# A graph network's own products moved into the aggregation, with input tiles and one-hots rearranged

## The reference

```python
x = ln(x + gcn_block(x))                 # W, degree norm, batch norm over nodes, gelu, + x
x = ln(x + sage(sage(x)))                # relu(h @ Ws + mean_of_neighbours(h) @ Wn + b), twice
x = ln(x + rgcn(relu(rgcn(x))))          # agg over edges of sigmoid(x_j @ gate_r) * x_j @ w_r, + x @ root + bias
x = ln(x + (relu((x + agg(x)) @ W1 + b1) @ W2 + b2))
# rgcn weights: w = einsum('rb,bio->rio', att, basis), 2 relations, 30 bases of 512 x 512
```

## Time and profile before

| | before |
|---|---|
| median of 3 runs, us | 933.22 (931.15 to 935.43) |
| the profiled execution, us | 935.52 |
| its span in the profile, us | 933.7 |
| TensorE matmul busy | 888.9 (95%) |
| VectorE busy | 668.8 (72%) |
| ScalarE busy | 280.8 (30%) |
| GpSimd busy | 85.5 (9%) |
| HBM read, written, MB | 97.80, 12.52 |

### The profile page before, as it was taken

How to read it: one execution, slowest core, us unless ns; L and a number is a source line. 1 busy time by engine, 2 the same in 40 slices (tenths; PEclk the granted TensorE clock), 3 DMA queues, 4 the chain that set the end, 5 groups by cost and what they waited for, 6 DMA issues and landing times.

```text
span 933.7 us, 12912 instructions
## 1 busy us (share of the span) xinstructions
PE 888.9 (95%) x4258; PEld 428.9 (46%) x4258; DVE 668.8 (72%) x1405; ACT 280.8 (30%) x431; POOL 85.5 (9%) x66
## 2 busy tenths in 40 slices
PE   7989999979987999989999899999999999999997
PEld 3544555535545544434444344444444444444443
DVE  6868888847996789798999988995324245552347
ACT  0323444633953213424132211113411131032321
...
GB/s 264 311 171 141 176 171 194 179 128 211 194 111 139 152 228 161 197 247 173 183 116 104 167 153 166 129 120 12 26 79 32 1 57 115 89 66 47 36 66 234
DMA packets 134889, 129.50 MB, mean 139 GB/s; under 512 B 80687, under 2 KB 81156, under 8 KB 134826
## 3 DMA queue, kind: packets, MB, share of 16 engines
...
...
HBM read 97.80 MB, written 12.52 MB: 118 GB/s over the span
## 4 chain that ended last, share of the span: by engine, by line
PE 61%; DVE 18%; DMA 7%; issue 5%; ACT 4%; DVEq 3%; POOL 1%; ACTq 0%; SPq 0%
PE Dp L667 25%; PE Dp L697 24%; PE T L621 6%; DVE acc L1252 4%; DMA stage<-in_basis 3%; PE Dp L573 3%; DVE Zraw L1141 2%; DMA wst<-mixd 2%; DVE Zraw L1140 1%; DVE Zraw L1363 1%; ACT W L1011 1%; PE T L667 1%; DVEq L1140 1%; ACT wst L864 1%; DVE w L1381 1%
## 5 line engine op out<-in xcount | busy, mean ns | idle before, releaser
L667 PE MATMUL Dp<-W,hT 128*128 128x512 f16 x792 | 176.2, 381 | 3.8 <-DMA hT<-S 3.8
L697 PE MATMUL Dp<-Zraw,A 128*128 128x512 f16 x800 | 173.0, 379 | 0.0
L1252 DVE SCALAR_TENSOR_TENSOR acc<-stage,att,acc 128x512 f32<-128x512 f32 x232 | 163.6, 769 | 6.2 <-DMA stage<-in_basis 6.2
L697 PE MATMUL Dp<-Zraw,AT 128*128 128x512 f16 x600 | 130.3, 379 | 0.3 <-DVE Zraw L1321 0.2
L667 PEld LDWEIGHTS Dp<-W,hT 128*128 128x128 f16 x792 | 77.7, 98 | 97.5 <-DMA hT<-S 4.6
L697 PEld LDWEIGHTS Dp<-Zraw,A 128*128 128x128 f16 x800 | 78.3, 98 | 94.4
L1141 DVE TENSOR_SCALAR Zraw<-hT,w 128x640 f16<-128x640 f16 (+1 forms) x209 | 96.4, 461 | 0.8 <-issue 0.7
L697 PEld LDWEIGHTS Dp<-Zraw,AT 128*128 128x128 f16 x600 | 58.6, 98 | 71.6 <-DVE Zraw L1321 0.7
L573 PE MATMUL Dp<-Zraw 128*128 128x320 f16 (+1 forms) x418 | 67.1, 307 | 9.2 <-DVE Zraw L1141 9.1
L1140 DVE TENSOR_SCALAR Zraw<-hT,w 128x128 f16<-128x128 f16 (+1 forms) x209 | 59.3, 284 | 22.1 <-issue 15.7
L1381 DVE SCALAR_TENSOR_TENSOR w<-Dp,aggc,S 128x512 f32<-128x512 f32 x40 | 29.9, 747 | 59.6 <-PE Dp L697 53.6
...
## 6 DMA issues: line engine op xcount, KB each, us to landing
...
```

The costliest lines, as they stand in the source:

```text
L667: last = nc.tensor.matmul(dense_bank(u, t, m), turned[:, hp, k * P:(k + 1) * P], weights_of(u, m)[:, wp, k, :], start=(n == 0), stop=(n == ...
L697: last = nc.tensor.matmul(sum_bank(t), a[:, k, ds(t * P, P)], Z[:, r, h, k, :], start=(n == 0), stop=(n == count - 1))
L1252: last = v.scalar_tensor_tensor(part, stage[:, q, :], a, part, ALU.mult, ALU.add)
```

## The change

1. Units 2 and 3 get `own_late`. Their own product leaves the dense part and is done tile by tile at the head of each tile's aggregation (`own_sum`, 12 matmuls into one of two banks of `T`). For it each tile is transposed a second time, into two slots (`fara`, `farb` in unit 2; `xra`, `xrb`, the residual's buffers, in unit 3), issued by ScalarE in `ln_step` or `relu_step`. VectorE adds the bias in `own_term`, in `after_agg`.
2. The basis quarters are dealt out anew: dense 2 from 18 to 8, agg 2 from 0 to 10, dense 3 from 35 to 24, agg 3 from 18 to 29.
3. In agg of unit 3 the maxima and scales of unit 4 are one tile later, as are the three `high` steps, so that the last one stands behind tile 9. The loads of biases 4 and 5 come one part later.
4. The input tiles are loaded one behind every two mixes instead of every three.
5. The low one-hots of a window's four fixed chunks are one instruction (`lows_of`), from an f16 copy of the low indices.
6. Transposed tiles 2 and 3 of unit 0 go to `xra` and `xrb` and no longer wait for the last mix; ScalarE issues them at the last window. One VectorE instruction (`eye`) waits on another semaphore.

The diff, cut to the changed lines and, in most places, the line ahead of them:

```diff
@@ -38,8 +38,8 @@
     dict(mats=["Wn1", "Ws1"], nz=1, own=1, zexp=18, bias="b1", ln=False),
-    dict(mats=["Wn2", "Ws2"], nz=1, own=1, zexp=24, bias="b2", ln=True),
-    dict(mats=["mix0", "mix1", "root1"], nz=2, own=2, zexp=18, bias="rb1", ln=False),
+    dict(mats=["Wn2", "Ws2"], nz=1, own=1, zexp=24, bias="b2", ln=True, own_late=True),
+    dict(mats=["mix0", "mix1", "root1"], nz=2, own=2, zexp=18, bias="rb1", ln=False, own_late=True),
@@ -157,8 +157,9 @@
         w_c = [zview(4 * NWIN).bitcast(f32) for _ in range(2)]
-        zview(2 * (2 * NT * D) - (2 * (KEYS + P) * (2 * OH + MORE) + 5 * 4 * NWIN))
+        lo_h = zview(2 * CHUNKS)
+        zview(2 * (2 * NT * D) - (2 * (KEYS + P) * (2 * OH + MORE) + 5 * 4 * NWIN + 2 * CHUNKS))
@@ -240,13 +241,14 @@
         s_wlo = sem("s_wlo")
-        s_hT = {n: sem(f"s_hT_{n}") for n in ("a", "b", "w1a", "w1b", "mida", "midb", "fara", "farb", "wsta", "wstb", "stga", "stgb")}
+        s_hT = {n: sem(f"s_hT_{n}") for n in ("a", "b", "w1a", "w1b", "xra", "xrb", "fara", "farb", "wsta", "wstb", "stga", "stgb")}
         s_own = {u: sem(f"s_own{u}") for u in (1, 2, 3, 4)}
+        s_od = sem("s_od")
@@ -330,14 +332,13 @@
             ("dense", 2, 8): [("load", 3, 2)],
-            ("agg", 2, 0): [("bias", 4)],
             ("agg", 2, 1): [("high", 3, 2)],
-            ("dense", 3, 1): [("gates", 2)],
+            ("dense", 3, 1): [("bias", 4), ("gates", 2)],
             ("dense", 3, 8): [("load", 4, 2)],
-            ("agg", 3, 1): [("bias", 5)],
-            ("agg", 3, 6): [("high", 4, 0)],
-            ("agg", 3, 7): [("high", 4, 1)],
-            ("agg", 3, 8): [("high", 4, 2)],
+            ("agg", 3, 7): [("high", 4, 0)],
+            ("agg", 3, 8): [("high", 4, 1)],
+            ("agg", 3, 9): [("high", 4, 2)],
+            ("dense", 4, 1): [("bias", 5)],
@@ -358,8 +359,8 @@
             ("agg", 3, 0): [("most", 4, 2)],
-            ("agg", 3, 5): [("most", 4, 0), ("most", 4, 1), ("max", 4)],
-            ("agg", 3, 6): [("scales", 4)],
+            ("agg", 3, 6): [("most", 4, 0), ("most", 4, 1), ("max", 4)],
+            ("agg", 3, 7): [("scales", 4)],
@@ -378,9 +379,10 @@
             ("agg", 1): [2, 2, 1, 1, 1, 2, 1, 2, 1, 1],
-            ("dense", 2): [1, 1, 2, 2, 2, 2, 2, 2, 2, 2],
-            ("dense", 3): [3, 4, 3, 4, 3, 4, 3, 4, 3, 4],
-            ("agg", 3): [4, 4, 4, 4, 2, 0, 0, 0, 0, 0],
+            ("dense", 2): [0, 1, 1, 1, 1, 1, 1, 1, 1, 0],
+            ("agg", 2): [1] * NT,
+            ("dense", 3): [2, 3, 2, 2, 3, 2, 2, 3, 2, 3],
+            ("agg", 3): [5, 4, 4, 4, 4, 4, 4, 0, 0, 0],
@@ -403,15 +405,16 @@
         far = Zraw[:, 4 * NT * D - 4 * D:]
-        mid = Zraw[:, 3 * NT * D:3 * NT * D + 4 * D]
-        HT_SLOT = {"mida": halves_view(mid[:, 0:2 * D]), "midb": halves_view(mid[:, 2 * D:]), "a": hT[:, 0], "b": hT[:, 1], "fara": halves_view(far[:, 0:2 * D]), "farb": halves_view(far[:, 2 * D:])}
-        for n, buffer in (("w1", w1), ("wst", wst), ("stg", stage)):
+        HT_SLOT = {"a": hT[:, 0], "b": hT[:, 1], "fara": halves_view(far[:, 0:2 * D]), "farb": halves_view(far[:, 2 * D:])}
+        for n, buffer in (("w1", w1), ("xr", xr), ("wst", wst), ("stg", stage)):
                 HT_SLOT[n + side] = halves_view(buffer[:, i, :].bitcast(f16))
-        HT_RING = {0: ["w1a", "w1b", "mida", "midb", "a", "b"], 2: ["a", "b", "fara", "farb"], 3: ["a", "b", "wsta", "wstb"],
+        HT_RING = {0: ["w1a", "w1b", "xra", "xrb", "a", "b"], 2: ["a", "b", "fara", "farb"], 3: ["a", "b", "wsta", "wstb"],
                     for u in range(NU) for t in range(NT)}
+        OWN_LATE = [u for u in range(NU) if UNITS[u].get("own_late")]
+        HT_NAMES.update({(u, NT + t): {2: "far", 3: "xr"}[u] + "ab"[t % 2] for u in OWN_LATE for t in range(NT)})
@@ -451,17 +454,17 @@
                 sp.dma_start(attp[b2 * 64:(b2 + 1) * 64, :], att1[b2:b2 + 1, :].broadcast_to([64, BASES])).then_inc(e_att, 16)
-            def load_mix(g, first=0, end=PAIRS):
-                for b in range(first, end):
-                    n = g * PAIRS + b
+            def load_mix(first, end):
+                for n in range(first, end):
+                    g, b = divmod(n, PAIRS)
-            load_mix(0, 0, MIX_FIRST)
+            load_mix(0, MIX_FIRST)
             sp.dma_start(src_i, src_t).then_inc(e_edge, 16)
-            load_mix(0, MIX_FIRST)
+            load_mix(MIX_FIRST, PAIRS)
@@ -470,12 +473,11 @@
             for t in range(NT):
-                load_mix(1 + t // 5, 3 * (t % 5), 3 * (t % 5) + 3)
+                load_mix(PAIRS + 2 * t, PAIRS + 2 * t + 2)
                 sp.dma_start(tile[:, :], vec).then_inc(s_bn, 16)
-            for mix_group in range(3, GROUPS):
-                load_mix(mix_group)
+            load_mix(PAIRS + 2 * NT, PAIRS * GROUPS)
@@ -640,7 +642,8 @@
             for u, unit in enumerate(UNITS):
-                nm, nz = len(unit["mats"]), unit["nz"]
+                own_late = unit.get("own_late", False)
+                nm, nz = len(unit["mats"]) - own_late, unit["nz"]
@@ -654,7 +657,7 @@
                         wait(pe, s_v, NT * LN.index(u) + t - 1)
-                    elif unit["own"] is not None:
+                    elif unit["own"] is not None and not own_late:
@@ -685,7 +688,9 @@
                     wait(pe, s_pre[u], bank_before(t))
-                    if unit["own"] is not None and t < 6:
+                    if own_late:
+                        own_sum(t)
+                    elif unit["own"] is not None and t < 6:
@@ -698,6 +703,21 @@
                     last.then_inc(s_agg[u], 1)
+                def own_sum(t):
+                    name = HT_NAMES[u, NT + t]
+                    pe.wait_ge(s_hT[name], 16 * (len(hT_before(u, NT + t)) + 1))
+                    wait(pe, s_own[u], t - 1)
+                    if t == 0:
+                        pe.wait_ge(s_wlo, halves_split(u))
+                    n, m = 0, unit["own"]
+                    for hp, wp in ((0, 0), (1, 0), (0, 1)):
+                        for k in range(KT):
+                            last = nc.tensor.matmul(T[:, t % 2, :], HT_SLOT[name][:, hp, k * P:(k + 1) * P],
+                                                    weights_of(u, m)[:, wp, k, :], start=(n == 0), stop=(n == 3 * KT - 1))
+                            n += 1
+                    last.then_inc(s_od, 1)
@@ -790,6 +810,8 @@
                             turned_out(t - 1, g, count_bank(t - 1, g))
+                    if w == NWIN - 1:
+                        turn_to(4, 0)
@@ -811,15 +833,19 @@
-                for t in range(turned[u], min(end, NT)):
+                count = 2 * NT if u in OWN_LATE else NT
+                for t in range(turned[u], min(end, count)):
                     slot = HT_NAMES[u, t]
-                    act.wait_ge(s_ready, NT * u + t + 1)
+                    act.wait_ge(s_ready, NT * u + min(t + 1, NT))
                     for before, tile in hT_before(u, t)[-1:]:
-                        act.wait_ge(s_d, NT * before + tile + 1)
-                    if slot[:2] == "w1" and t < 2:
+                        if tile < NT:
+                            act.wait_ge(s_d, NT * before + tile + 1)
+                        else:
+                            act.wait_ge(s_od, NT * OWN_LATE.index(before) + tile - NT + 1)
+                    if u == 3 and t in (NT, NT + 1):
+                        act.wait_ge(s_v, NT * (LN.index(2) + 1))
+                    if slot[:2] in ("w1", "xr") and t < 4:
                         act.wait_ge(s_ready, NT)
-                    elif slot[:3] == "mid" and t < 4:
-                        act.wait_ge(s_mx, PAIRS * GROUPS)
@@ -827,15 +853,15 @@
                     act.dma_start_transpose(HT_SLOT[slot].rearrange("p h (k n) -> p (h k) n", k=KT),
-                                            S16[:, t, :]).then_inc(s_hT[slot], 16)
-                turned[u] = max(turned[u], min(end, NT))
+                                            S16[:, t % NT, :]).then_inc(s_hT[slot], 16)
+                turned[u] = max(turned[u], min(end, count))
...
                 else:
-                    act.wait_ge(x_hi, NT)
+                    act.wait_ge(s_d, NT)
@@ -926,6 +952,8 @@
                 def ln_step(t, j):
+                    if u in OWN_LATE and t:
+                        turn_to(NT + t + 2, u)
@@ -943,7 +971,9 @@
                     if t:
-                        turn_to(t + (4 if u else 6), u)
+                        turn_to(min(t + (4 if u else 6), NT), u)
+                    if u in OWN_LATE and t == NT - 2:
+                        turn_to(NT + 2, u)
@@ -970,6 +1000,8 @@
                         act.wait_ge(s_xst[u - 2][j], 8 * NT)
+                    if u == 4:
+                        act.wait_ge(s_od, 2 * NT)
@@ -992,8 +1024,10 @@
                 def relu_step(t, j):
+                    if u == 3 and t:
+                        turn_to(NT + t + 2, u)
                     if t > 2:
-                        turn_to(min(t - 2, 4), u + 1)
```

(40 more changed lines are left out.)

13 lines of the change are left out of this document (6 added, 7 removed).

## The result

The changed kernel takes 960.91 us (median of 4 runs, 958.45 to 963.28) beside 932.18 for the kernel before in the same comparison (930.58 to 935.43): ratio 1.0298, 95% interval 1.0273 to 1.0322. It is slower, as forecast, but by 28.7 us where 14.0 were forecast, and it lies above the range of 930 to 956. Its profiled execution took 958.45 with a span of 956.6. TensorE's matmul busy time is 892.7 (93% of it), VectorE's 658.4, ScalarE's 280.6, GpSimd's 88.1, and HBM read and written are the same to the last digit. TensorE issues as many matmuls as before (4258) and stands idle for longer.

A forecast was written before the change was run, and what follows sets the result against it. TensorE was taken as nearly full from dense 2 to agg 3, with ScalarE's queue and transpose landings limiting the moved products. Late part +24.5 and early part -10.5 gave +14.0 on 933.2: 947 us, range 930 to 956.

The forecast's parts named there:

- What bounds the kernel: Dense 2 to agg 3: TensorE has 260 us of work in 272.6, so only about 12.5 us can be won.
- Input tiles: Window stage: earlier input tiles remove TensorE's gaps, 8.1 us, less 1.5 charged for delayed mix slices: net -6.6.
- (c): Window stage: early input tiles starve the mix, early part -3.4 alone, total 954; chance 0.13.
- Two places: Start of dense 0: transposed tiles 2 and 3 land before TensorE asks, so its wait goes: net -3.4 us.
- Low one-hots: Window stage: the single instruction takes 0.69 us, VectorE wins nothing; -0.5 us for fewer issues.
- Dense 2: Unit 2's dense: ScalarE's queue sets its end; agg starts at 443.6, 10.1 us earlier for 26.0 us of work removed.
- Agg 2: Unit 2's aggregation: output, store, transpose landing (3.5) and matmuls form a loop, 7.9 us a tile instead of 6.93.
- Dense 3 and agg 3: Unit 3: the gates' gap of 4.92 goes, TensorE's own work sets the pace, and agg ends at 687.7.
- Dense 4: Start of unit 4: its third weights' split, now after agg 3's last tile, ends late; 4.4 us of new gap.
- (a): Agg 2: transposes land in time, 7.03 us a tile; late part +15.5, total 938; chance 0.18.
- (b): Dense 2: ScalarE's queue is no limit, dense ends near 430; late part about -1, total 922; chance 0.09.
- (d): Units 2 and 3: moved own products take and cost no idle time; late 0 to +6, total 923 to 929; chance 0.08.

The follow-up runs named there:

- e_weights_later: The changed kernel with the split of unit 3's first weights behind dense 2's last tile, the next loads and splits in agg 2: 961.2 us, ratio 1.0312.
- e_no_quarters: The changed kernel with the ten basis quarters of agg 2 back in dense 2 (18 there, as before): 959.72 us, ratio 1.0291.
- e_lows: The kernel before with only the low one-hots of a window in one instruction: 928.24 us, ratio 0.995.
- e_issue_first: The changed kernel with unit 2's own-tile transposes issued one step sooner, at the head of ScalarE's step in agg 2: 945.34 us, ratio 1.0123.

## Why the prediction was right or wrong

- **What bounds the kernel.** It held: no more than about 12.5 us of idle time could be won between dense 2 and agg 3, and no variant of the move won anything there.
- **Input tiles: right.** -6.6 forecast, -7.2 measured. The charge of 1.5 for starved mix slices was not needed; rival (c) fell, as TensorE is full from 20 to 40 us at a DMA share of 1.05.
- **Two places: right.** -3.4 forecast, -3.1 measured.
- **Low one-hots: wrong, a mis-sized term.** -0.5 forecast, -4.5 measured. The price of the instruction was right (0.69 us). I counted "0.5 for fewer issues" without looking at how long VectorE stood for issue before these instructions: 15.7 us over the stage, of which 7.1 went. And I valued VectorE's time at nothing because the stage seemed to be TensorE's, although TensorE's own small gaps named VectorE. The Trainium skill, "Vector Engine (DVE) Microarchitecture Reference", section 5.1, which gave one result per cycle for this form, agrees with the trace here: with f16 output, 512 results took 0.69 us, as the slope of 1.04 ns each in the earlier trace rows gives, and not 0.42. The step from there to "worth nothing" was mine.
- **Dense 2: right in size, and in the main in mechanism.** Agg 2 was to start at 443.6; 426.42 + 18.8 is 445.2. ScalarE's queue sets it, and e_weights_later shows it by taking 11.3 us out. It missed by 1.6 us. One reading in it was wrong: the basis quarters were said not to be last there, but with all 18 left in dense 2 (e_no_quarters) it lasts 55.96 instead of 50.23, so VectorE and its loads were close to last too, and most of the 8.5 won hangs on the quarters' move. Matmuls behind gaps ran slowly, which I had not priced: the twelve at 388.21 took 5.28 us at a granted clock of 0.50 (1.2 GHz), and the stretch as a whole has 0.86.
- **Agg 2: right mechanism, mis-sized.** 7.9 us a tile forecast, 9.1 measured from tile 3 on; agg 2 took 88.05 where 79.5 were forecast, +8.5. The term that failed is the landing: "I take 3.5, towards the low end because fewer loads run beside it". The row gave a median of 3.9, and the chain 5.66, 4.7 and 4.1. The reason was wrong too: every tile of agg 2 now has a basis quarter beside it, and e_no_quarters, without them, shows a median of 3.7 for 4.7. The row was also taken where no weights are loaded; in dense 2 of the kernel before, five transposes issued from 413 to 431 took 4.9 to 12.4 us. The second is the clock: I priced own sum and aggregation at 6.93 while I forecast a gap before each, and the matmuls behind such gaps took 4.45 instead of 2.75. It had been seen in the earlier trace rows, and it stood only in the upper bound. In the cycle read above these two are 2.2 and 1.7 of the 4.3 us too many. Over the three rounds from own tile 3 to own tile 9 (56.2 us where 47.4 were forecast) and the last tile, the landings are 4.0 and the clock 3.4 of the 8.8 too many.
- **Dense 3 and agg 3: nearly.** 164.6 forecast, 168.6 measured. The gates' gap didn't go entirely (2.08), and VectorE waited for a basis load, which gave the new one (1.81).
- **Dense 4: right gap, clock forgotten.** 4.48 for 4.4; the following matmuls cost another 2.4 (dense 4 takes 84.52 where it took 77.70).
- **The sum.** Late: +1.6, +8.5, +4.0, +2.4 over 24.5 is 41.0, as the traces have it (-18.8 at dense 2, +22.5 at agg 4: 41.3). Early: -16.4 instead of -10.5. By the medians the late parts cost 28.7 + 16.4, 45.1; the two traces are only 22.9 apart where the medians are 28.7, and show 41.3 of it. The upper bound of the late part was +28, 3.5 above its forecast; that is room for landing (1.4) and clock (1.7) about once each, but they recur from tile to tile, and the measured late cost lies far outside its bounds. The direction was forecast rightly, but it was luck that the total missed by no more: the early parts won 5.9 us more than forecast, which hid a part of the 20.6 by which the late ones cost more.
- **The signs.** Of those named, the gap by GpSimd (4.48) and the gap of 3.59 came as told, and agg 2 began where forecast once the lead of 18.8 is taken off. Its tiles were 9.1 apart, not 7.7 to 8.2, and dense 0 started 13.1 us earlier, not 8 to 12; the low one-hots alone bring 5.7 of it (192.18 in e_lows).
- **The rivals.** (a) and (b) fell in this kernel, yet (a) is what e_issue_first makes true: the transposes land in time and the pace is TensorE's. (c) fell with the input tiles. (d) fell: the move alone costs 45.
